# One core: products of probabilities and values taken one 64-key block at a time on the two halves of the array, with several moves of work between queues

## The chip, the core and the metric

The kernel runs on one core of a Trainium2 chip. The metric is the device time of one execution in microseconds (us). Before the change, three timed runs gave 854.46, 857.27 and 858.67 us, a median of 857.27 us. The profile is of one further execution, which took 856.18 us. The engines are called as in the profile: PE (matrix products; PEld is its weight load), DVE (vector), ACT (scalar), POOL (GpSimd) and SP, which here only issues DMAs and waits. "SPq" rows are what SP's own sequencer does, so a row `SPq L387 DMA_DIRECT2D` is the issue of one DMA, not its transfer.

## The reference, cut to what it computes

The input has 4096 tokens of 256 numbers (8 sequences of 512). First comes an attention over `ctx` in blocks of 64: a query sees only the 64 keys of its own block, in each of 16 heads of 16 numbers. Then comes a mixture of 8 experts, of which each token uses its best 2.

```python
x = x + _L0_xattn_ref(_layernorm(x, axis=-1), ctx_1024, ctx_1024, ...)
    scores = jnp.einsum('bhqd,bhkd->bhqk', q, k) / jnp.sqrt(jnp.float32(dk))
    bid = jnp.arange(s) // BLOCK_SIZE            # 64
    attn_mask = jnp.where(bid[:, None] == bid[None, :], 0.0, NEG)
    attn = jax.nn.softmax(scores + attn_mask, axis=-1)
    x = jnp.einsum('bhqk,bhkd->bhqd', attn, v)
    return x.transpose(0, 2, 1, 3).reshape(b, s, d) @ Wo + bo
x = x + _L0_ffn_ref(_layernorm(x, axis=-1), ...)
    weights = softmax(x @ gate_w.T + expert_bias); top_w, top_i = top_k(weights, 2)
    for e in range(8):
        h = gelu(x @ w_up[e].T); y = h @ w_down[e].T
        out = out + sparse_w[..., e:e+1] * y
    out = layernorm(out)
    return out + x
```

## The kernel before

**Two stages.** The tokens are 32 tiles of 128. The first stage is a pipeline over *steps*: in step i, each engine works on several tiles at once (the first number after `here(j, u, ...)` is the skew: tile i + skew). Steps 6 to 13 are a loop in hardware; the rest is written out. After the steps come 39 *items*: an item is 256 token rows of one expert, gathered through DRAM.

**One step on PE**, in order: transposes of the next tile (L452), scores of tile i (L464, on 64 rows at a time), transposes of the probabilities of tile i-1 (L474), the projections of q and k of tile i+1 (L486, L491), L499, the product of probabilities and values of tile i-1 (L507), the transposes of `xn2` of tile i-3 (L517), the projection of v of tile i (L529), the output projection (L544) and the gate's logits (L557).

L507 takes one pair of heads for both 64-key blocks of a tile at once: all 128 keys are contracted, and the values tile `v_x` holds each block's values in columns of its own, with zeros in the rows of the other block. Each product gives 66 columns, in fp32.

**One step on DVE**, in order: L807 (adds the output projection), L814 (statistics of the input tile i+3), L819, L825, L832, L839 (the second normalisation's mean and variance), L847 and L853 (maximum and difference of the scores), L861 and L869 (`xn` and `xn2`, two `tensor_scalar`), L878 (k for the next tile), L886 (`ctx_lo`, the low half of the context, which PE's L529 waits for), L893 and four L898 (division by the sum). In steps 15 to 33 parts of the routing follow (`route`).

**ACT** writes, among others, the scaled weights (L1007, L1022), `prob_t` (L1012), `ctx_hi` (L1017), q (L1031), the exponential (L1036) and the values into `v_x` (two L1059, one for each block).

**POOL** waits for L839, makes reciprocal roots (L1106, L1108), adds the output bias (L1136), makes L1140 and then the low half of a weight tile (L1144, 128x1024, which also waits for ACT's L1022), and later scatters rows (L1115).

**SP's queue**, one step: the input tile i+3 (L373, waited for by L814; here called the *x load*), the context and weights of tile i+1, row loads for the scatter, and the write of `xn2` of tile i-3 to `xn_rows` (L387, which waits for L869). SP issues in this order, and a wait holds everything behind it.

**Rows to the experts.** Each row of `xn_rows` has 256 numbers and, in column 256, the row's place. All 8192 places are written by one DMA on ACT's queue at the start (L987). For each tile, `row_in` loads two blocks of 128 rows from `xn_rows` into a ring of buffers `xr` (RING = 4), and POOL scatters each to `x_sorted`; a ring buffer is free again when its scatter has landed.

**The items.** The order of the items is decided in three rounds (tiles 0 to 10, 11 to 21, 22 to 31): item 0 may be loaded when the tiles up to 10 are scattered, item 3 when those up to 21 are, and item 7 when all are and nine blocks of zeros (the *pads*) are written. Item loads (L411), pads (L419, L420) and row loads (L367) all stand in SP's queue. On PE, `moe(k)` is: transposes of item k+2 (L572), `up` of item k+1 (L589, four quarters), `down` of item k (L605). A quarter of `up` for one item may be written when ACT's gelu (L1080) has read that quarter of the item before. The third round's counts (`read_counts(2)`, `place_rows(2)`, needed by the scatter of tiles 22 to 31) stand on DVE behind the four gelu quarters of item 0.

## Time and profile before

| what | before |
|---|---|
| profiled execution | 856.18 us, span of the trace 854.4 us |
| median of three timed runs | 857.27 us |
| PE busy | 734.5 us (86% of the span) |
| PEld busy | 655.7 us (77%) |
| DVE busy | 541.0 us (63%) |
| ACT busy | 389.6 us (46%) |
| POOL busy | 339.0 us (40%) |
| mean granted PE clock | 0.935 of full |

The span is the time from the first to the last instruction of the core; 1.8 us of the device time lie outside it. Busy shares are averages over stages with different limits, so they must be read by stretch. A group of the rows below gives the start in us, the duration in us, the engine, the line and the operation with its tiles; in square brackets stands how long the engine had been idle and what ended that.

### The profile page before, as it was taken

How to read it: one execution, taken by the hardware profiler on the slowest of the kernel's cores; microseconds unless marked ns; L12 is line 12 of the kernel's file. 1: busy time of each engine (PE TensorE's matmuls, PEld its weight loads, DVE VectorE, ACT ScalarE, POOL GpSimd, SP SyncE). 2: the span in 40 equal slices, each digit the busy share in tenths (PEclk: the TensorE clock that was granted, in tenths of full speed). 3: DMA queues.
4: the chain of work that ended last, by engine and by line, in shares of the span. 5: the costliest groups of instructions: out<-in, count | busy, mean ns of one | idle time of the engine just before them, and what ended most of it. 6: DMA issues, size and time to landing. Idle time of an engine off the chain costs nothing.

```text
span 854.4 us, 19926 instructions
## 1 busy us (share of the span) xinstructions
PE 734.5 (86%) x6340; PEld 655.7 (77%) x6340; DVE 541.0 (63%) x1292; ACT 389.6 (46%) x747; POOL 339.0 (40%) x500
## 2 busy tenths in 40 slices
PE   4788888889888888627968999999999999999990
PEld 4778887878777777416856998989988999999980
DVE  3576777786778777519425555555666667766662
ACT  3777778776667657212122222222333334433441
POOL 3344455444456455634535111111333334433453
PEclk9899999988989979858989999999999999999995
DMA  9234434333344553554673111112222233333222
GB/s 157 75 101 107 122 99 112 103 101 97 100 133 135 148 143 106 132 152 132 195 168 111 50 50 45 51 51 76 74 83 82 87 101 101 105 94 99 83 87 92
DMA packets 74090, 88.46 MB, mean 104 GB/s; under 512 B 15440, under 2 KB 64976, under 8 KB 74000
## 3 DMA queue, kind: packets, MB, share of 16 engines
q1 hardware_dynamic: 58112, 67.21, 29.2%
q0 software_dynamic: 6816, 18.65, 5.9%
q10 hardware_dynamic: 9072, 1.39, 1.8%
q8 instruction: 57, 0.93, 0.5%
q14 instruction: 33, 0.27, 0.1%
HBM read 53.63 MB, written 33.63 MB: 102 GB/s over the span
## 4 chain that ended last, share of the span: by engine, by line
PE 28%; issue 12%; POOL 9%; DMA 7%; SPq 2%; DVE 2%; ACT 0%; POOLq 0%; DVEq 0%
PE ps_a L589 13%; PE ps_b L605 13%; POOL y_rows L1176 4%; DMA area<-xn_rows 3%; DMA x_sorted<-area,slot_row 3%; POOL tiny L1163 2%; PE ps_c L572 1%; POOL x_sorted L1115 1%; DMA area<-x_sorted 1%; POOL tiny L1170 1%; POOL tiny L1165 1%; POOL tiny L1160 1%; DMA xn_rows<-area 1%; SPq L418 0%; SPq L419 0%
## 5 line engine op out<-in xcount | busy, mean ns | idle before, releaser
L589 PE MATMUL ps_a<-area,weights_s 128*128 128x256 f16 x1872 | 217.3, 277 | 1.9 <-DVE area L927 1.6
L605 PE MATMUL ps_b<-weights_s,area 128*128 x1872 | 210.6, 273 | 0.1
L589 PEld LDWEIGHTS ps_a<-area,weights_s 128*128 x1872 | 185.9, 100 | 26.6 <-issue 2.9
L605 PEld LDWEIGHTS ps_b<-weights_s,area 128*128 128x128 f16 x1872 | 183.1, 98 | 21.5 <-issue 0.3
L1080 ACT ACTIVATE area<-ps_a 128x512 f32<-128x512 f32 x156 | 92.6, 597 | 115.7 <-PE ps_a L589 112.7
L1176 POOL DMA_INDIRECT y_rows<-weights_s,tiny x78 | 85.9, 1101 | 127.3 <-ACT weights_s L1087 100.8
L1087 ACT ACTIVATE weights_s<-ps_b 128x512 f32<-128x512 f32 x39 | 23.3, 598 | 193.5 <-PE ps_b L605 165.6
L961 DVE SCALAR_TENSOR_TENSOR area<-area 128x512 f16<-128x512 f32 x156 | 108.0, 692 | 5.3
L1115 POOL DMA_INDIRECT x_sorted<-area,slot_row x64 | 66.2, 1034 | 54.3 <-DMA area<-xn_rows 41.2
L959 DVE TENSOR_SCALAR area<-area 128x512 f16<-128x512 f32 x156 | 66.5, 426 | 21.4 <-ACT area L1080 20.3
L1144 POOL TENSOR_TENSOR weights_s<-weights_s 128x1024 f16<-128x1024 f32 (+1 forms) x32 | 68.9, 2152 | 28.1 <-ACT weights_s L1022 27.8
L1106 POOL TENSOR_TENSOR area<-area,tiny 128x1 f32<-128x1 f32 x64 | 12.4, 193 | 149.9 <-DVE area L839 130.7
L925 DVE TENSOR_SCALAR area<-ps_c 128x512 f16<-128x512 f32 x39 | 26.9, 689 | 68.9 <-PE ps_c L572 68.9
L964 DVE SCALAR_TENSOR_TENSOR resid<-area,tiny,resid 128x256 f32<-128x256 f32 x32 | 15.5, 484 | 75.2 <-ACT resid L1092 75.0
L507 PE MATMUL ps_b<-area 128*128 128x66 f32 x512 | 61.0, 272 | 1.8 <-ACT area L1012 1.8
L507 PEld LDWEIGHTS ps_b<-area 128*128 128x128 f32 x512 | 59.7, 192 | 2.3 <-ACT area L1012 2.3
L1160 POOL TENSOR_TENSOR tiny<-tiny 128x1 f32<-128x1 f32 x32 | 7.5, 234 | 134.9 <-DVE tiny L975 134.9
L529 PE MATMUL ps_a<-area 128*128 128x256 f16 x192 | 30.1, 299 | 31.6 <-DVE area L886 31.6
L572 PE MATMUL ps_c<-cst,area 128*128 128x128 f32 x156 | 25.4, 289 | 31.6 <-DMA area<-x_sorted 31.6
L1031 ACT ACTIVATE area<-ps_c,tiny,cst 128x128 f32<-128x128 f32 x128 | 48.0, 460 | 6.4 <-PE ps_c L491 6.4
L878 DVE SCALAR_TENSOR_TENSOR area<-ps_c,cst 128x256 f32<-128x256 f32 x64 | 27.9, 477 | 36.3 <-issue 23.5
L529 PEld LDWEIGHTS ps_a<-area 128*128 128x128 f16 x192 | 17.5, 104 | 41.7 <-DVE area L886 39.1
(145 smaller groups left out, 1167.1 us busy)
## 6 DMA issues: line engine op xcount, KB each, us to landing
weights_s<-weights SPq DMA_DIRECT2D x32, 512.0 KB, 4.1
area<-x_sorted SPq DMA_DIRECT2D x39, 257.0 KB, 2.8
area<-xn_rows SPq DMA_DIRECT2D x64, 128.5 KB, 3.5
xn_rows<-area SPq DMA_DIRECT2D x32, 256.0 KB, 3.5
area<-y_rows SPq DMA_DIRECT2D x32, 256.0 KB, 2.9
resid<-x_in SPq DMA_DIRECT2D x32, 128.0 KB, 3.6
area<-ctx_t SPq DMA_DIRECT2D x32, 128.0 KB, 2.5
out<-resid SPq DMA_DIRECT2D x32, 128.0 KB, 2.8
```

The costliest lines, as they stand in the source:

```text
L507: mm = pe.matmul(ps_o[:, h // 4, (h % 4) * NB:(h % 4 + 1) * NB, :], prob_t[:, h, :], v_x[:, h // HC, h % HC, :, :], start=True, stop=True)
L529: mm = pe.matmul(ps_v, c[:, k, :], w[:, k, :], start=(n == 0), stop=(n == 3 * HC - 1))
L572: mm = pe.transpose(ps_x[:, b, at:at + P], xg[b][:, v, c * P:(c + 1) * P], ident)
L589: mm = pe.matmul(ps_h[:, q, (ic % 2) * SLOTS:(ic % 2 + 1) * SLOTS], weights_s[:, bass.ds(first + ((2 * hc + part) * WCOLS + ic * P), P)], ...
L605: mm = pe.matmul(ps_y[:, b, v * D:(v + 1) * D], g[b][:, ic, v * P:(v + 1) * P], weights_s[:, bass.ds(first + (col + part * WCOLS), D)], st ...
L959: dve.tensor_scalar(g_hi[b][:, c, :], src, G_SCALE, None, ALU.mult).then_inc(gh_r, 1)
L961: dve.scalar_tensor_tensor(g_lo[b][:, c, :], src, G_SCALE, g_hi[b][:, c, :], ALU.mult, ALU.subtract).then_inc(gl_r, 1)
L1031: act.activation(q_m[:, c, :, h, :], ps_q[:, c].rearrange("p (b q) -> p b q", b=NB), ACT.Identity, bias=bq_m[:, c, h:h + 1], scale=cst[:, ...
L1080: act.activation(g_s[q], ps_h[:, q, :], ACT.Gelu, scale=1.0 / (X_SCALE * W_SCALE)).then_inc(g_r, 1)
L1115: pool.indirect_dma_start(x_sorted[:, :], bass.IndirectOffsetOnAxis(ap=slot_row[:, m % TOPK, n:n + 1], axis=0), xr[s], None).then_inc(rsc[ ...
L1144: pool.tensor_tensor(w_part(t, 1), w_stage(t), w_part(t, 0), ALU.subtract).then_inc(w_lo_r, 1)
L1176: pool.indirect_dma_start(y_rows[:, :], bass.IndirectOffsetOnAxis(ap=y_at[k % 4][:, v:v + 1], axis=0), y_s[k % 2][:, v * D:(v + 1) * D], N ...
```

## The change

It has these parts.

1. L507's product is taken per block: 16 products of 64 keys and 33 columns instead of 8 of 128 keys and 66 columns, block 0 on the upper and block 1 on the lower 64 rows of the array, each into its own PSUM bank. `v_x` has half the columns and no zeros, so ACT fills it with one instruction in place of two (L1059), DVE divides with two 64x256 instructions in place of four 64x128 (L898), and the first memset is small.
2. `ctx_hi` (L1017) comes first in ACT's step, and `ctx_lo` (L886) moves on DVE from behind L878 to in front of L847.
3. The places of the rows are no longer written by one DMA at the start, but tile by tile: a DMA of 256 numbers of 4 bytes on SP's queue behind each L387.
4. The item loads move from SP's to ACT's queue (`load_item`), items 0 and 1 into step 34, and item k+4 between the second and third gelu of item k+1. SP issues all row loads up to tile 31 first, then the pads.
5. RING is 3, and the pads' zeros have a buffer of their own.

```diff
-RING = 4
+RING = 3
...
-        v_x = carve(PAIRS * NB * VCOLS).rearrange("p (s c b x) -> p s c b x", s=STRIPS, c=HC, b=NB)
+        v_x = carve(PAIRS * VCOLS).rearrange("p (s c x) -> p s c x", s=STRIPS, c=HC)
...
+        pad_zero = carve(ROW)
...
                 for m, s, uses in loads_of(n):
                     since(sp, rsc[s], 16 * uses)
-                    if m == 0:
-                        sp.wait_ge(at_out, 16)
-                    sp.wait_ge(xn2_out[n % 2], 16 * (n // 2 + 1))
+                    sp.wait_ge(xn2_out[n % 2], 32 * (n // 2 + 1))
...
                     sp.dma_start(xn_by_tile.rearrange("(c t) p d -> t p c d", c=TOPK)[bass.ds(t, 1), :, :, 0:D].rearrange("a p c d -> p (a c) d"),
                                  xn2.unsqueeze(1).to_broadcast([P, TOPK, D])).then_inc(xn2_out[b], 16)
+                    sp.dma_start(xn_by_tile.rearrange("(c t) p d -> t p c d", c=TOPK)[bass.ds(t, 1), :, :, D:ROW].rearrange("a p c d -> p (a c) d"),
+                                 route_consts[:, R_AT:R_END].rearrange("p (c t) -> t p c", c=TOPK)[bass.ds(t, 1)].rearrange("a p c -> p (a c)").unsqueeze(2),
+                                 allow_slow_non_contiguous=True).then_inc(xn2_out[b], 16)
...
-            x_units = x_sorted.rearrange("(s v p) d -> s p v d", v=SUBS, p=P)
+            for n in range(17, TILES):
+                row_in(n)
...
             def moe(k):
-                i = k + 4
-                if item_valid(i):
-                    b = i % 2
-                    if i in ROUND_OF:
-                        r = ROUND_OF[i]
-                        sp.wait_ge(items_r, r + 1)
-                        rows_scattered(sp, sum(ROUNDS[r][0:2]))
...
-                for n in {-2: (17, 18, 19, 20, 21), -1: (22, 23), 0: (24, 25, 26), 1: (27, 28, 29, 30, 31)}.get(k, ()):
-                    row_in(n)
...
                     for h in range(PAIRS):
-                        mm = pe.matmul(ps_o[:, h // 4, (h % 4) * NB:(h % 4 + 1) * NB, :], prob_t[:, h, :],
-                                       v_x[:, h // HC, h % HC, :, :], start=True, stop=True)
+                        for n in range(NB):
+                            r = slice(n * BLOCK, (n + 1) * BLOCK)
+                            mm = pe.matmul(ps_o[:, n, h, :], prob_t[r, h, :], v_x[r, h // HC, h % HC, :], start=True, stop=True)
...
                 t, half, b = here(j, u, 0)
                 if valid(t):
+                    dve.wait_ge(ctx_hi_r, t + 1)
+                    since(dve, v_ps, t)
+                    dve.scalar_tensor_tensor(ctx_lo, ctx[b], CTX_SCALE, ctx_hi, ALU.mult, ALU.subtract).then_inc(ctx_lo_r, 1)
+
+                t, half, b = here(j, u, 0)
+                if valid(t):
                     since(dve, sub_r, t)
...
-            act.dma_start(xn_rows.rearrange("(g p) d -> p g d", p=P)[:, :, D:ROW], route_consts[:, R_AT:R_END].unsqueeze(2),
-                          allow_slow_non_contiguous=True).then_inc(at_out, 16)
...
+            def load_item(i):
+                b = i % 2
+                if i in ROUND_OF:
+                    r = ROUND_OF[i]
+                    act.wait_ge(items_r, r + 1)
+                    rows_scattered(act, sum(ROUNDS[r][0:2]))
+                    if r == 0:
+                        act.wait_ge(k_ps, TILES)
+                    if r == 2:
+                        act.wait_ge(padded, 16 * (E + 1))
+                since(act, gt_ps, i - 1)
+                since(act, at_r, i - 1)
+                at_x = act.value_load(item_x[0:1, i:i + 1], min_val=0, max_val=SPARE)
+                act.dma_start(xg[b], x_units[bass.ds(at_x, 1)].rearrange("a p v d -> p (a v) d")).then_inc(xgot[b], 16)
...
+                if isinstance(j, int) and 2 * j + u == 34:
+                    load_item(0)
+                    load_item(1)
...
                     for q in range(GQ):
+                        if q == 2 and item_valid(k + 4):
+                            load_item(k + 4)
                         act.wait_ge(h_ps, GQ * i + 1 + q)
```

Line numbers of the changed kernel differ by a few from those of before. In SP's queue, in the written-out steps, this stood between the write of `xn2` (L387) and the x load of the next step (L373):

```order
L377 DMA area<-ctx_t 128x256
L381 DMA weights_s<-weights 128x1024
L387 DMA xn_rows<-area 128x2x256
L373 DMA resid<-x_in 128x256
L377 DMA area<-ctx_t 128x256
```

and this stands there now (L385 is the write of `xn2`, L387 the DMA of the places, L371 the x load):

```order
L375 DMA area<-ctx_t 128x256
L379 DMA weights_s<-weights 128x1024
L385 DMA xn_rows<-area 128x2x256
L387 DMA xn_rows<-route_consts 128x2x1
L371 DMA resid<-x_in 128x256
L375 DMA area<-ctx_t 128x256
```

One DMA has come between the two, and nothing else. On DVE, one step before, from L839 on:

```order
L839 BN_AGGR area<-area 128x2
L847 TENSOR_REDUCE area<-ps_a 128x16
L853 TENSOR_TENSOR area<-ps_a,area 128x1024
L861 TENSOR_SCALAR area<-resid,area 128x256
L869 TENSOR_SCALAR area<-resid,area,rs_all 128x256
L878 SCALAR_TENSOR_TENSOR area<-ps_c,cst 128x256 x2
L886 SCALAR_TENSOR_TENSOR area<-area 128x256
L893 RECIPROCAL area<-ps_b 128x16
L898 TENSOR_TENSOR area<-ps_b,area 64x128 x4
```

and the same step now (L820 is the former L839, L828 the former L886, L856 the former L869):

```order
L820 BN_AGGR area<-area 128x2
L828 SCALAR_TENSOR_TENSOR area<-area 128x256
L834 TENSOR_REDUCE area<-ps_a 128x16
L840 TENSOR_TENSOR area<-ps_a,area 128x1024
L848 TENSOR_SCALAR area<-resid,area 128x256
L856 TENSOR_SCALAR area<-resid,area,rs_all 128x256
L865 SCALAR_TENSOR_TENSOR area<-ps_c,cst 128x256 x2
L874 RECIPROCAL area<-ps_b 128x16
L878 TENSOR_TENSOR area<-ps_b,area 64x256 x2
```

`ctx_lo` has moved in front of the two score operations, so that one more instruction stands between the former L839, for which POOL waits, and the former L869. On ACT, from the loading of gelu's table on, the first items now read so (L1078 is a gelu quarter, L983 and L984 an item load; the first load there is item 2's, the next item 3's, the last item 4's):

```order
L1065 ACT_TABLE_LOAD
L1065 ACTIVATE tiny<-tiny 128x1
L983 TENSOR_LOAD item_x
L983 ISA x2
L984 ISA
L984 DMA area<-x_sorted 128x2x257
L1078 ACTIVATE area<-ps_a 128x512 x2
L983 TENSOR_LOAD item_x
L983 ISA x2
L984 ISA
L984 DMA area<-x_sorted 128x2x257
L1078 ACTIVATE area<-ps_a 128x512 x4
```

Before, the gelu quarters of items 0 and 1 stood there with nothing between them, and ACT had no item load:

```order
L995 ACTIVATE area<-area 128x80
L1071 ACT_TABLE_LOAD
L1071 ACTIVATE tiny<-tiny 128x1
L1080 ACTIVATE area<-ps_a 128x512 x8
L1087 ACTIVATE weights_s<-ps_b 128x512
L1080 ACTIVATE area<-ps_a 128x512 x4
```

## Rows read from the trace of the kernel before

**Rows 1.** Windows: us; busy PE, PEld, DVE, ACT, POOL; PE clock, DMA share, GB/s.

```profile
600.00:700.00 100.00, 100.00 (x918) 90.03 (x916) 64.63 (x139) 35.55 (x65) 32.74 (x57) 1.00 0.29 86
```

**Rows 2.** Timeline of PE, from 92 to 102 us (steps of the loop).

```profile
92.14 0.83 PE L529 MATMUL ps_a<-area 128*128 128x256 f16 x6 [1.10 <-DVE area L886]
...
94.38 1.16 PE L464 MATMUL ps_a<-area 64*128 64x128 f32 x16
...
98.41 1.90 PE L507 MATMUL ps_b<-area 128*128 128x66 f32 x16
100.15 0.39 PE L517 MATMUL ps_a<-cst,area 128*128 128x128 f32 x2
101.64 0.83 PE L529 MATMUL ps_a<-area 128*128 128x256 f16 x6 [1.11 <-DVE area L886]
```

**Rows 3.** Timeline of DVE, the same steps.

```profile
94.98 0.43 DVE L814 BATCH_NORM_STATS2 area<-resid 128x6 f32 x1 [0.17 <-DMA resid<-x_in]
...
96.06 0.18 DVE L839 BATCH_NORM_AGGREGATE area<-area 128x2 f32<-128x6 f32 x1 [0.17 <-issue]
...
98.89 0.41 DVE L869 TENSOR_SCALAR area<-resid,area,rs_all 128x256 f32 x1
...
101.11 0.48 DVE L886 SCALAR_TENSOR_TENSOR area<-area 128x256 f16<-128x256 f32 x1
```

**Rows 4.** Timeline of SP's queue, the same steps.

```profile
89.87 0.41 SPq L387 DMA_DIRECT2D xn_rows<-area  x1
90.51 0.35 SPq L373 DMA_DIRECT2D resid<-x_in  x1
```

**Rows 5.** Timeline of POOL, the same steps.

```profile
96.32 0.19 POOL L1106 TENSOR_TENSOR area<-area,tiny 128x1 f32<-128x1 f32 x1 [4.52 <-DVE area L839]
...
99.17 2.13 POOL L1144 TENSOR_TENSOR weights_s<-weights_s  x1
```

**Rows 6.** Timeline of ACT, the same step.

```profile
97.53 0.41 ACT L1017 ACTIVATE area<-area 128x256 f16<-128x256 f32 x1
```

**Rows 7.** Timeline of DVE, 262 to 284 us (written-out steps with routing).

```profile
264.15 2.22 DVE L869 TENSOR_SCALAR area<-resid,area,rs_all 128x256 f32<-128x256 f32 x1
...
270.49 0.43 DVE L814 BATCH_NORM_STATS2 area<-resid 128x6 f32<-128x256 f32 x1 [0.39 <-DMA resid<-x_in]
```

**Rows 8.** Timeline of POOL, the same stretch.

```profile
264.01 2.20 POOL L1144 TENSOR_TENSOR weights_s<-weights_s 128x1024 f16<-128x1024 f32 x1
```

**Rows 9.** Timeline of SP's queue, the same stretch.

```profile
266.40 0.40 SPq L387 DMA_DIRECT2D xn_rows<-area  x1
```

**Rows 10.** Groups by line and shape: busy us, mean ns, idle before.

```profile
L869 DVE TENSOR_SCALAR area<-resid,area,rs_all 128x256 f32<-128x256 f32 x24 | 22.5, 940 | 3.2 <-POOL rs_all L1108 1.9 <-DMA xn_rows<-area 1.3
```

**Rows 11.** DMA queues of the page: packets, MB, share of 16 engines over the span.

```profile
q10 hardware_dynamic: 9072, 1.39, 1.8%
```

**Rows 12.** Timeline of PE, transposes of items 0, 3 and 7.

```profile
377.76 1.09 PE L572 MATMUL ps_c<-cst,area 128*128 128x128 f32 x4 [15.55 <-DMA area<-x_sorted]
...
405.91 1.12 PE L572 MATMUL ps_c<-cst,area 128*128 128x128 f32 x4 [5.72 <-DMA area<-x_sorted]
...
466.06 0.60 PE L572 MATMUL ps_c<-cst,area 128*128 128x128 f32 x4
```

**Rows 13.** Timeline of SP's queue, row loads of tiles 13 to 16, and pads.

```profile
360.81 11.45 SPq L367 DMA_DIRECT2D area<-xn_rows  x8
...
420.27 9.61 SPq L419 DMA_DIRECT2D x_sorted<-weights_s  x8
```

**Rows 14.** Chain that ended last, 388 to 402 us: row loads and scatters in turn.

```profile
388.84 2.38 DMA area<-xn_rows
...
391.48 5.40 DMA x_sorted<-area,slot_row
396.90 2.23 DMA area<-xn_rows
...
399.40 2.60 DMA x_sorted<-area,slot_row
```

More of the change, by code:

```diff
@@ L471, in step @@
                     pe.wait_ge(p_r, t + 1)
-                    since(pe, o_r, 4 * t)
+                    since(pe, o_r, 2 * t)
                     for h in range(PAIRS):
@@ L514, in rows_for_gate @@
                         since(pe, x2t_r, t)
-                        since(pe, v_r, 2 * (min(t + 3, TILES) if isinstance(t, int) else t + 3))
+                        since(pe, v_r, min(t + 3, TILES) if isinstance(t, int) else t + 3)
                         for c in range(HC):
@@ L524, in step @@
                     pe.wait_ge(ctx_lo_r, t + 1)
-                    since(pe, v_r, 2 * t)
+                    since(pe, v_r, t)
                     n = 0
@@ L645, in _ @@
         def _(dve):
-            dve.memset(v_x, 0.0).then_inc(zeroed, 1)
-            dve.wait_ge(zeroed, 1)
-            for n in range(NB):
-                r = slice(n * BLOCK, (n + 1) * BLOCK)
-                ins = dve.memset(v_x[r, :, :, n, 2 * DK:VCOLS].rearrange("p s c x -> p (s c) x"), 1.0)
-            ins.then_inc(zeroed, 1)
+            dve.memset(v_x.rearrange("p s c x -> p (s c) x")[:, :, 2 * DK:VCOLS], 1.0).then_inc(zeroed, 1)
             links = [0]
@@ L866, in step @@
                     dve.wait_ge(rs2_r, t + 1)
-                    since(dve, xn2_out[1 - b], 16 * (half + b))
+                    since(dve, xn2_out[1 - b], 32 * (half + b))
                     since(dve, x2t_ps, t)
@@ L880, in step @@
                                                  ALU.add, ALU.mult).then_inc(k_r, 1)
-                t, half, b = here(j, u, 0)
-                if valid(t):
-                    dve.wait_ge(ctx_hi_r, t + 1)
-                    since(dve, v_ps, t)
-                    dve.scalar_tensor_tensor(ctx_lo, ctx[b], CTX_SCALE, ctx_hi, ALU.mult, ALU.subtract).then_inc(ctx_lo_r, 1)
                 t, half, b = here(j, u, -1)
@@ L997, in step @@
             def step(j, u):
+                t, half, b = here(j, u, 0)
+                if valid(t):
+                    act.wait_ge(ctx_in[b], 16 * (half + 1))
+                    since(act, v_ps, t)
+                    act.activation(ctx_hi, ctx[b], ACT.Copy, scale=CTX_SCALE).then_inc(ctx_hi_r, 1)
                 t, half, b = here(j, u, 1)
@@ L1012, in step @@
                     act.activation(prob_t, ps_pt, ACT.Copy).then_inc(pt_r, 1)
-                t, half, b = here(j, u, 0)
-                if valid(t):
-                    act.wait_ge(ctx_in[b], 16 * (half + 1))
-                    since(act, v_ps, t)
-                    act.activation(ctx_hi, ctx[b], ACT.Copy, scale=CTX_SCALE).then_inc(ctx_hi_r, 1)
                 t, half, b = here(j, u, 0)
@@ L1056, in step @@
                     since(act, o_ps, t)
[L1057 to L1061 removed]
+                    act.activation(v_x[:, :, :, 0:2 * DK], ps_v.rearrange("p (c s d) -> p s c d", c=HC, s=STRIPS),
+                                   ACT.Copy, scale=1.0 / (CTX_SCALE * W_SCALE)).then_inc(v_r, 1)
             step(-1, 1)
```

46 lines of the change are left out of this document (15 added, 31 removed).

## The prediction

> **What bounds the kernel now.** The windows come first. In the items, PE is busy for all of a stretch of 100 us [rows 1]; an item costs it 100 records (48 up, 48 down, 4 transposes), so 918 records in 100 us are 10.9 us an item, and nothing in the change touches that work. What can move is the attention stage (to about 360 us), the passage to the items (360 to 466 us), and, where they end later or sooner, the end by as much.
>
> The timelines of one step come next, engine by engine. On PE a step of the loop takes 9.50 us (92.14 to 101.64), and 1.11 us of it is a wait for L886 [rows 2]. PE's own part is thus 8.39 us. A second circle runs beside it. SP writes `xn2` (L387 at 89.87), and behind it issues the x load (90.51) [rows 4]; L814 begins at 94.98, and its bracket says that it waited for that load, 5.11 us after L387's issue [rows 3]. From L814 to L839 are 1.08 us, from L839 to L869 2.83 us [rows 3], then 0.41 us for L869 itself and some 0.1 us until SP issues the next L387. The sum is 5.11 + 1.08 + 2.83 + 0.41 + 0.1 = 9.5 us. **Two circles of the same length bound a step**, and the change shortens only the first.
>
> In the passage I read PE's transposes. Item 0's came at 377.76 after 15.55 us of waiting for its rows, item 3's at 405.91 after 5.72 us, and from item 7's, at 466.06, PE runs on [rows 12]. SP issued the row loads of tiles 13 to 16 from 360.81 to 372.3, with item 0's load behind them, and from 420.27 spent 9.61 us on pads [rows 13].
>
> **The change, part by part.** *PE's product.* L507 takes 1.74 us from its start to L517's (98.41 to 100.15), for 16 records on the full array [rows 2]. The new form has 32 records on half the rows. Bounds: if pairs run side by side, no more than now; if they follow each other like the 16 records of L464 (1.16 us, also on 64 rows), 2.32 us, 0.6 more. I take +0.4. PE's circle is then 8.8 us without the wait for L886. This is hidden as long as the other circle is longer; without that cover it costs 0.4 us a step.
>
> *`ctx_lo` earlier.* L886 no longer holds PE. On DVE it now stands between L839 and L869, so the second circle gets longer by its place: 0.48 us as it stands at 101.11 [rows 3], 0.3 if the part in which it waited is taken off. I take 0.4.
>
> *The places, tile by tile.* The new DMA stands between L387 and the x load, so the x load is issued later by one issue; L387 to the x load was 0.64 us [rows 4], which is the upper bound, and nothing is the lower one, if the x load waits for L387's data anyway. Its 256 packets go over 16 engines. ACT's queue, with 9072 packets, nearly all of this kind, used 1.8% of 16 x 854.4 us [rows 11], at most 27 ns each, so 16 packets take 0.43 us. Together 0.4 to 1.1 us; I take 0.7. The Trainium skill (DMA: Bandwidth & Descriptors, section Queues, rings and completion order) says that a DMA's semaphore increment lands only after every earlier write of that engine; by it the x load could not be seen before the 4-byte writes are done, the upper end of this term. No row here has both DMAs, so the sum goes by 0.7.
>
> So the second circle becomes 9.5 + 0.4 + 0.7 = 10.6 us against 9.5. In the 8 steps of the loop that is 1.1 x 8 = **+9 us** (5.5 to 12). In the written-out steps with an x load and without routing (4, 5, 14 to 16) SP needs fewer instructions of its own; I take 0.8 x 5 = **+4** (0 to 6). In the 12 with routing DVE's own work mostly covers the x load (one waited 0.39 us [rows 7]); I take **+2** (0 to 10).
>
> *L869 against L1144.* In a step at 264 us POOL's L1144 began at 264.01 [rows 8] and L869, at 264.15, took 2.22 us in place of 0.41 [rows 7]. L869's 24 written-out instances are busy 22.5 us [rows 10]: (22.5 - 24 x 0.41) / 1.81 = 7 such cases. Where L869 begins first, as at 98.89 against 99.17 [rows 3, 5], it is not held. The Trainium skill (SBUF — State Buffer, section Who interferes with whom) states the rule: one port pair is shared by the two, and whichever starts first keeps it for the whole instruction. The trace agrees, with 0.14 us one way and 0.28 the other. What becomes of the 0.28 us? L869 moves back by 0.4 (L886 in front). L1144 moves forward by 0 to 0.3, where it waited for L1022, since L1017 (0.41 us [rows 6]) no longer stands ahead of that. And L886 now reads at the time of POOL's L1106, 0.26 us behind L839 [rows 3, 5], which can push POOL's chain back by 0 to 0.4. L1144 thus begins between 0.42 before and 0.28 behind L869, nearer to before. I take 11 of the 17 written-out steps with an x load, where 6 were held. A held L869 delays L387 and so the x load by 1.8, of which 1.5 is left: 5 x 1.5 = **+7.5** (from -11, all gone, to +28, all 25 steps).
>
> *Start and end of the stage.* Nine steps without such an x load lose their wait for L886, at most 1.1 us each; DVE and ACT follow closely, so I take half: **-4** (-10 to 0).
>
> *The passage.* Item 0's load now waits only for tile 10, so PE can begin at about 362.2 (377.76 - 15.55). But item 3's load stands on ACT in front of item 0's third gelu and holds it until all tiles up to 21 are scattered. A ring buffer's turn (load, scatter) took 8.04 us (388.84 to 396.88) and 5.10 us (396.90 to 402.00) [rows 14]; I take the mean, 6.6, with three buffers 2.2 us a block. The 18 blocks of tiles 13 to 21 from 361.3 end near 402. PE then stands in the middle of `up` of item 1; half an `up` (2.6), a `down` (5.2) and 1.5 to get going put item 3's transposes at 411.5, against 405.91. Further, DVE's third counts stand behind the same gelu, about 7.5 us later by the lengths of the instructions between, so the scatter of tile 22 begins at 409.5. Of its 20 blocks three are loaded already and 17 follow at 2.2: SP is done at 447. The pads come after that (10 us of issues, 5 to land): item 7 can be loaded at 462. ACT waits for it in front of item 4's third gelu, so half an `up`, a `down` and the cold start, 10.5 us, lie ahead of item 7's transposes: 472.5 against 466.06, **+6.5**. With turns of 5.10 throughout it is -11, with 8.04 +23.
>
> *At nothing.* One ACT and two DVE instructions fewer a tile lie beside the x load. The 39 item loads on ACT, about 1 us each, are covered in the items, where ACT is busy 35.55 of 100 us [rows 1]; without that cover they would hold gelu. The memset and the DMA of places at the start have no engine waiting for them in the first steps.
>
> **Sum**, against the profiled 856.2 us: 856.2 + 9 + 4 + 2 + 7.5 - 4 + 6.5 = 881.2. The median of the runs lies 1.1 us above the profiled one, so about **882**.
>
> **Rivals.** *The x load is in time* (faster). The second circle is the time from L387 to the x load's landing, plus 0.4 + 1.08 + 2.83 + 0.41 + 0.1 = 4.8. If the landing takes 4.0 us, places included, PE's 8.8 bounds. In favour: at 270.49 L814 saw the load 4.09 us after the L387 of 266.40 [rows 7, 9]; against: 5.11 in the loop [rows 3, 4]. Then 13 steps gain 0.7 (-9), the 12 with routing 0.3 for the shorter DVE (-4), the ends -4, the passage stays at +6.5, and no held L869 is added: 845.7, or **847**. It decides from a landing of 4.7 us downward, where the circle falls under 9.5.
>
> *L869 is held everywhere* (much slower), also in the loop: 25 held instead of 6 give 19 x 1.5 = 28.5 in place of 7.5, **903**. In favour: the order above; against: in the loop L1144 was bounded by POOL's own chain, which L886 can only push back.
>
> *It nets out* (same). Landing at 4.7 and a ring that turns in 6 us: no term of the steps but -4, and the passage at +4: **857**.
>
> **Chances.** The forecast 0.57 (867 to 894, by its terms' bounds), x load in time 0.17, all held 0.13, nets out 0.13. Half a per cent, 4.3 us, is about what a measurement of this kernel can tell from no change. So faster 0.17, same 0.13, slower 0.70. The range for 8 in 10 is 850 to 896: it takes in "nets out", all of the forecast but its edge, and the nearer parts of the two outer cases.
>
> **What would show it.** Right: L814's idle time named by the x load in most steps of the loop; no wait of L529 for L886's successor; loop steps of 10.2 to 11 us; more than 7 L869 over 2 us; PE's transposes of item 0 near the end of the stage, then a gap of some 25 us before the middle of item 1's `up`, ended by ACT. Wrong: L814 without waits and steps of 9 us; or a gap in item 1 so short that item 7's transposes come no later after the stage's end than before (106 us).

## The result, and the profile after

The changed kernel takes 917.56 us (median of 4 runs, 915.03 to 919.65), the kernel before 857.97 us in the same session. The ratio is 1.0695 [1.0646, 1.0745]: about 60 us slower, where 25 us were forecast. The profiled execution after has a span of 917.8 us against 854.4, 63 us more.

I divide these 63 us by two instants of each trace. The last `xn2` copy (L869, now L856) ends at 359.97 us before and at 409.18 after: **the attention stage lost 49 us** (forecast 18.5). From there to the transposes of item 7 were 106.1 us and are now 120.4: **the passage lost 14 us** (forecast 6.5). From item 7 on both kernels need 388 us.

Windows after, columns as in [rows 1], and two windows of before beside them:

```profile
42.00:190.00 148.00, 125.17 (x1096) 110.29 (x1095) 97.25 (x192) 85.72 (x168) 55.12 (x86) 0.82 0.39 86
190.00:360.00 170.00, 146.43 (x1268) 129.89 (x1266) 126.17 (x292) 100.17 (x196) 75.79 (x108) 0.81 0.47 106
600.00:700.00 100.00, 100.00 (x918) 90.04 (x917) 57.77 (x116) 30.43 (x54) 22.65 (x34) 1.00 0.21 63
```

```profile
42.00:190.00 148.00, 128.71 (x1141) 117.19 (x1142) 110.08 (x291) 113.89 (x228) 68.25 (x106) 0.98 0.38 107
190.00:360.00 170.00, 142.08 (x1109) 126.11 (x1106) 129.77 (x351) 107.76 (x216) 87.18 (x125) 0.89 0.45 123
```

The items are untouched (918 records in 100 us, as in [rows 1]). In the attention stage DVE, ACT and POOL are busy for less of the same time. PE is busy for nearly as long as before, but its granted clock (third number from the right) is 0.82 and 0.81 where it was 0.98 and 0.89.

One step of the loop on DVE after, then POOL and SP's queue in the same stretch (compare [rows 3 to 5]):

```profile
115.68 0.18 DVE L820 BATCH_NORM_AGGREGATE area<-area 128x2 f32<-128x6 f32 x1 [0.17 <-issue]
...
117.39 1.22 DVE L840 TENSOR_TENSOR area<-ps_a,area 128x1024 f32<-128x1024 f32 x1
118.53 2.33 DVE L848 TENSOR_SCALAR area<-resid,area 128x256 f32 x1
120.78 0.40 DVE L856 TENSOR_SCALAR area<-resid,area,rs_all 128x256 f32 x1
...
127.76 0.43 DVE L795 BATCH_NORM_STATS2 area<-resid 128x6 f32 x1 [2.25 <-DMA resid<-x_in]
...
129.03 0.43 DVE L828 SCALAR_TENSOR_TENSOR area<-area 128x256 f16<-128x256 f32 x1
129.37 1.22 DVE L834 TENSOR_REDUCE area<-ps_a 128x16 f32<-128x1024 f32 x1
130.62 1.22 DVE L840 TENSOR_TENSOR area<-ps_a,area 128x1024 f32<-128x1024 f32 x1
```

```profile
117.75 0.73 POOL L1132 TENSOR_TENSOR resid<-resid,area 128x256 f32 x1
118.43 0.20 POOL L1136 TENSOR_TENSOR mr_all<-area,rs_all 128x1 f32 x1
118.57 2.13 POOL L1140 TENSOR_TENSOR weights_s<-weights_s  x1
```

```profile
121.34 0.41 SPq L385 DMA_DIRECT2D xn_rows<-area  x1
122.02 0.62 SPq L387 DMA_DIRECT2D xn_rows<-route_consts  x1
123.48 0.35 SPq L371 DMA_DIRECT2D resid<-x_in  x1
```

The same copy before, and the small POOL instruction that ran beside it:

```profile
98.57 0.41 DVE L861 TENSOR_SCALAR area<-resid,area 128x256 f32 x1
```

```profile
98.69 0.34 POOL L1140 TENSOR_TENSOR mr_all<-area,rs_all 128x1 f32 x1
```

The step is 13.23 us long (117.39 to 130.62). L848, the former L861, takes 2.33 us in place of 0.41, and ends 0.16 us behind POOL's L1140 (120.86 and 120.70). The x load is issued 2.14 us behind L385, with the places between them, and L795 waits 2.25 us for it: 6.42 us after L385 instead of 5.11 [rows 3, 4].

Groups by line and shape over the whole execution (busy us, mean ns, idle before), with PE's two below:

```profile
L848 DVE TENSOR_SCALAR area<-resid,area 128x256 f32<-128x256 f32 x24 | 30.5, 1273 | 0.0
L856 DVE TENSOR_SCALAR area<-resid,area,rs_all 128x256 f32<-128x256 f32 x24 | 18.6, 774 | 5.6 <-DMA xn_rows<-route_consts 3.7 <-POOL rs_all L1104 1.9
L848 DVE TENSOR_SCALAR area<-resid,area 128x256 f32 x8 | 12.8, 1603 | 0.0
L795 DVE BATCH_NORM_STATS2 area<-resid 128x6 f32<-128x256 f32 x24 | 10.2, 425 | 32.2 <-DMA resid<-x_in 25.1 <-issue 7.0
L795 DVE BATCH_NORM_STATS2 area<-resid 128x6 f32 x8 | 3.4, 427 | 11.8 <-DMA resid<-x_in 11.8
```

```profile
L494 PE MATMUL ps_b<-area 64*128 64x33 f32 x1024 | 65.4, 279 | 1.8 <-ACT area L1011 1.8
L503 PE MATMUL ps_a<-cst,area 128*128 128x128 f32 x64 | 17.8, 369 | 49.8 <-DVE area L856 49.8
```

Of the 64 copies of L848 and L856, 23 took over 1 us, 17 of them L848; before it was 8 of 64, seven of them L869 [rows 10]. PE now waits 49.8 us for L856, in front of L503. Its wait for the `ctx_lo` copy, in front of L515, is gone.

The passage: PE's transposes of items 0, 3 and 7; SP's queue; the item loads and what follows on ACT.

```profile
411.83 1.08 PE L558 MATMUL ps_c<-cst,area 128*128 128x128 f32 x4 [0.42 <-issue]
...
462.25 0.60 PE L558 MATMUL ps_c<-cst,area 128*128 128x128 f32 x4
...
529.60 0.60 PE L558 MATMUL ps_c<-cst,area 128*128 128x128 f32 x4
```

```profile
410.78 88.92 SPq L365 DMA_DIRECT2D area<-xn_rows  x38
500.77 9.39 SPq L404 DMA_DIRECT2D x_sorted<-area  x8
510.20 0.47 SPq L405 DMA_DIRECT2D x_sorted<-area  x1
```

```profile
451.18 0.39 ACTq L984 DMA_DIRECT2D area<-x_sorted  x1
451.61 2.06 ACT L1078 ACTIVATE area<-ps_a 128x512 f32<-128x512 f32 x4 [31.12 <-issue]
...
517.60 0.39 ACTq L984 DMA_DIRECT2D area<-x_sorted  x1
```

Item 0 starts 2.7 us after the stage, where 2.2 were forecast, and then ACT stands 31 us in front of item 3's load. The pads leave only behind all 38 row loads, and item 7's load (517.60) behind the pads.

### The profile page after: what moved, and what is told of

The parts are those of the page before. It is cut to its first block, busy times and chain, and to the rows that moved or that the text cites. A ratio compares the mean times of both kernels' runs of the same rounds, so it can differ in the third digit from the quotient of the medians.

```text
span 917.8 us, 20908 instructions
## 1 busy us (share of the span) xinstructions
PE 773.6 (84%) x6852; PEld 685.9 (75%) x6852; DVE 562.7 (61%) x1226; ACT 377.3 (41%) x715; POOL 337.7 (37%) x500
## 4 chain that ended last, share of the span: by engine, by line
PE 26%; issue 12%; DMA 9%; POOL 8%; DVE 2%; SPq 1%; ACT 0%; ACTq 0%; POOLq 0%; DVEq 0%
PE ps_b L591 12%; PE ps_a L575 12%; POOL y_rows L1172 4%; DMA x_sorted<-area,slot_row 4%; DMA area<-xn_rows 4%; POOL tiny L1159 1%; PE ps_c L558 1%; POOL tiny L1166 1%; DMA x_sorted<-area 1%; POOL tiny L1161 1%; POOL tiny L1156 1%; POOL x_sorted L1111 1%; SPq L403 0%; DVE area L856 0%; SPq L404 0%
## 5 line engine op out<-in xcount | busy, mean ns | idle before, releaser
L1078 ACT ACTIVATE area<-ps_a 128x512 f32<-128x512 f32 x156 | 90.3, 596 | 176.7 <-PE ps_a L575 68.4
L1172 POOL DMA_INDIRECT y_rows<-weights_s,tiny x78 | 84.8, 1087 | 142.6 <-ACT weights_s L1083 118.4
L1102 POOL TENSOR_TENSOR area<-area,tiny 128x1 f32<-128x1 f32 x64 | 16.7, 260 | 202.9 <-DVE area L820 185.0
L1111 POOL DMA_INDIRECT x_sorted<-area,slot_row x64 | 63.5, 993 | 58.7 <-DMA area<-xn_rows 38.4
L1140 POOL TENSOR_TENSOR weights_s<-weights_s 128x1024 f16<-128x1024 f32 (+1 forms) x32 | 68.4, 2136 | 19.6 <-ACT weights_s L1016 19.4
L494 PEld LDWEIGHTS ps_b<-area 64*128 64x128 f32 x1024 | 61.7, 193 | 7.2 <-issue 4.8
L494 PE MATMUL ps_b<-area 64*128 64x33 f32 x1024 | 65.4, 279 | 1.8 <-ACT area L1011 1.8
L943 DVE SCALAR_TENSOR_TENSOR resid<-area,tiny,resid 128x256 f32<-128x256 f32 x32 | 15.5, 484 | 75.3 <-ACT resid L1088 75.2
L503 PE MATMUL ps_a<-cst,area 128*128 128x128 f32 x64 | 17.8, 369 | 49.8 <-DVE area L856 49.8
L1011 ACT ACTIVATE area<-ps_b 128x1024 f32<-128x1024 f32 x32 | 32.8, 1024 | 45.2 <-PE ps_b L459 45.2
L530 PE MATMUL ps_a<-area 128*128 128x256 f32 x128 | 48.0, 515 | 1.0 <-ACT area L1041 1.0
L449 PE MATMUL ps_a<-area 64*128 64x128 f32 x512 | 47.3, 337 | 1.7 <-issue 1.7
```

The costliest lines, as they stand in the source:

```text
L449: mm = pe.matmul(ps_a[:, a].rearrange("p (s x k) -> p x s k", s=2, k=BLOCK)[:, c * NB + n], q_m[r, c, n].rearrange("p h q -> p (h q)"), k_ ...
L494: mm = pe.matmul(ps_o[:, n, h, :], prob_t[r, h, :], v_x[r, h // HC, h % HC, :], start=True, stop=True)
L530: mm = pe.matmul(ps_wo_last if last_out(t) else ps_wo, o_t[:, h, :], wo_s[:, h, :], start=(h == 0), stop=(h == 1))
L1078: act.activation(g_s[q], ps_h[:, q, :], ACT.Gelu, scale=1.0 / (X_SCALE * W_SCALE)).then_inc(g_r, 1)
L1111: pool.indirect_dma_start(x_sorted[:, :], bass.IndirectOffsetOnAxis(ap=slot_row[:, m % TOPK, n:n + 1], axis=0), xr[s], None).then_inc(rsc[ ...
L1140: pool.tensor_tensor(w_part(t, 1), w_stage(t), w_part(t, 0), ALU.subtract).then_inc(w_lo_r, 1)
```

## The experiments

Each ratio is to runs of the kernel before on the same chip, so it is the ratios that are compared between chips. "Held" counts the copies to `xn` and `xn2` that took over 1 us, of 64; "stage" is the end of the last copy to `xn2`; "cold" is the number of the 32 steps in which the four records of PE's output projection (L530 in the changed kernel) took over 1.4 us together, up to 2.1, instead of 1.0 to 1.1; "passage" is as above. These four come from one execution of each kernel. Executions of one kernel differ: the kernel before took 846.1 to 856.8 us on one chip, and the one traced took 856.2. So a few us between two traces show nothing by themselves.

| kernel | ratio to before | held | stage | cold | passage |
|---|---|---|---|---|---|
| before | 1 | 8 | 360.0 | 6 | 106.1 |
| changed | 1.0695 [1.0646, 1.0745] | 23 | 409.2 | 18 | 120.4 |
| `e1_places` | 1.0435 [1.0383, 1.0486] | 28 | 386.7 | 15 | 114.2 |
| `e2_ctx` | 1.0484 [1.0395, 1.0573] | 15 | 389.7 | 12 | 114.2 |
| `e3_both` | 1.0305 [1.0250, 1.0359] | 6 | 371.9 | 13 | 116.8 |
| `e4_poolwait` | 1.0167 [1.0107, 1.0226] | 1 | 362.9 | 10 | 112.6 |
| `e7_halves` | 1.0131 [1.0049, 1.0213] | 8 | 377.3 | 13 | 105.7 |
| `e5_xearly` | 1.0261 [1.0161, 1.0362] | 27 | 373.6 | 12 | 120.4 |
| `a_both` | 0.9864 [0.9788, 0.9941] | 1 | 330.6 | 2 | 120.4 |
| `e9_passage` | 1.0186 [1.0108, 1.0263] | 9 | 359.9 | 4 | 119.0 |
| `c_pads` | 0.9701 [0.9635, 0.9766] | 1 | 316.9 | 1 | 115.2 |
| `c_cures_sp` | 0.9491 [0.9441, 0.9541] | 1 | 315.1 | 2 | 102.1 |
| `b_both` | 0.9971 [0.9935, 1.0007] | 0 | 358.2 | 7 | 102.9 |
| `b_poolwait` | 0.9987 [0.9952, 1.0022] | 0 | 354.2 | 7 | 102.2 |

**Parts 2 and 3 undone, apart and together.** Part 3 undone takes the second DMA out and puts the one at the start back:

```diff
-                    sp.dma_start(xn_by_tile...[bass.ds(t, 1), :, :, D:ROW]..., ...).then_inc(xn2_out[b], 16)
...
+            act.dma_start(xn_rows...[:, :, D:ROW], route_consts[:, R_AT:R_END].unsqueeze(2), ...).then_inc(at_out, 16)
```

> The changed kernel (917.6 us) with part 3 undone: the places again in one DMA at the start on ACT's queue. Theory 1 (the port: what was lost in the attention stage is mostly that L848 or L856 is held by POOL's L1140, in 20 steps against 8 before, 1.9 us each, because ctx_lo now stands in front of L834): the x load lands 0.7 us sooner in each of 24 steps, and the held steps stay, 20 of 32 within 4: 897 to 905. Theory 2 (the late x load: the stage was lengthened by the second DMA between the xn2 write and the x load): 25 to 35 us come back, 883 to 893, and the idle time of L795 for the x load falls from 36.9 us to under 8.

Part 2 undone moves the blocks of `ctx_lo` (here) and `ctx_hi` back, without a change in them:

```diff
-                    dve.scalar_tensor_tensor(ctx_lo, ctx[b], CTX_SCALE, ctx_hi, ALU.mult, ALU.subtract).then_inc(ctx_lo_r, 1)
...
                     dve.tensor_reduce(row_max, ps_s, AX.X, ALU.max).then_inc(max_r, 1)
...
+                    dve.scalar_tensor_tensor(ctx_lo, ctx[b], CTX_SCALE, ctx_hi, ALU.mult, ALU.subtract).then_inc(ctx_lo_r, 1)
...
                     dve.wait_ge(o_ps, t + 1)
```

> The changed kernel with part 2 undone: ctx_hi behind prob_t on ACT and ctx_lo behind L878 on DVE, as before. Theory 1 (the port): held copies fall from 20 to about 8, and the path from L795 to L856 loses the 0.43 us of ctx_lo: 12 x 1.9 + 24 x 0.4 = 32 us back, 882 to 892. Theory 2 (the late x load): only the 0.4 us per step come back, 905 to 912, and the held copies stay about as many. PE waits for ctx_lo again in both.

`e3_both` has both edits.

> The changed kernel with parts 2 and 3 undone, so with the product by halves, the item loads on ACT and the ring of three. Both theories: the attention stage is as long as before within 5 us (last L856 at 355 to 365 us), and what is left over 858 is the passage, 14 us: 866 to 876. If it stays over 880, the product by halves costs in the attention stage too.

`e1_places` gave back 2.6% (some 22 us), between the two theories; `e2_ctx` gave back 2.1% (18 us), less than theory 1 wanted. The counts say why neither explains the loss alone. With `ctx_lo` in front of L834 and the old places, 28 copies are held, nearly one in every step; with the new places and `ctx_lo` at its old place still 15; with both undone 6. **Each part by itself brings copies under L1140**: 28 and 15 are held, and 6 with neither part. Together they give back 3.9%, and the rest, 1.0305, lies above what both theories allowed (866 to 876 us, at most 1.021): the stage is still 12 us longer, and PE cold in 13 steps, with nothing left of the change in it but the half product. That led to `e7_halves`.

**The port alone.** POOL's L1140 is made to wait until DVE is through L856; nothing is undone.

```diff
                     pool.wait_ge(w_hi_r, t + 1)
+                    since(pool, xn2_r, t - 2)
```

> The changed kernel, all parts kept, with one wait more: POOL's L1140 (the low part of a weight slice) waits for L856 of the same step, so that it never runs beside L848 and L856. Theory 1 (the port): none of the 64 copies is held any more, up to 20 x 1.9 = 38 us back, of which some is eaten where PE or the x load bounds the step next: 880 to 895. Theory 2 (the late x load): a held copy only uses up time in which the x load would be waited for anyway, so under 8 us come back: 910 to 918.

From 1.0695 to 1.0167, some 45 us, more than the 38 expected; between the two profiled executions the stage is 46 us shorter (409.2 to 362.9). Theory 2, by which under 8 us come back, is out. But the x load is late here too: L795 still waits for it 21 times, 41.5 us in all. One step of the loop on DVE, and POOL's instruction that now comes behind L856:

```profile
119.03 0.40 DVE L848 TENSOR_SCALAR area<-resid,area 128x256 f32 x1
119.35 0.41 DVE L856 TENSOR_SCALAR area<-resid,area,rs_all 128x256 f32 x1
...
125.73 0.43 DVE L795 BATCH_NORM_STATS2 area<-resid 128x6 f32 x1 [0.79 <-DMA resid<-x_in]
...
129.66 0.40 DVE L848 TENSOR_SCALAR area<-resid,area 128x256 f32 x1
```

```profile
120.12 2.13 POOL L1141 TENSOR_TENSOR weights_s<-weights_s  x1 [0.98 <-DVE area L856]
```

The step is 10.63 us (119.03 to 129.66). The prediction's sum of the second circle, held copies left out, was 10.6.

**The x load a step earlier**, so that it no longer stands behind the `xn2` write and the places:

```diff
-                t, half, b = here(j, u, 3)
+                t, half, b = here(j, u, 4)
                 if valid(t):
                     since(sp, x_in[b], 16 * half)
...
-            for i in range(-3, 0):
+            for i in range(-4, 0):
```

> The changed kernel, all parts kept, with each x load issued one step earlier, ahead of the xn2 write and the places instead of behind them. Theory 1 and 2 together (the circle through the x load is what bounds a step): L795 no longer waits for it (36.9 us before), and the step falls to the circle of L856, L503, L530, L543, L788 and L795, 4.4 + 6.5 = 10.9 us where a copy is held: 25 to 35 us less than the changed kernel, ratio to before 1.03 to 1.04. If the x load's lateness were only what fills a wait on PE, under 8 us come back.

1.0261, a little better than expected: L795 waits twice for the x load, 4.3 us in all. A copy is still held in 27 cases, and a step of the loop is 10.64 us (L848 at 100.18 and 110.82), near the 10.9 expected of the circle through L503. The late x load was real: 36 us of the stage (409.2 to 373.6), not much less than the 46 of the other cure. The trace is of the longest of the four executions, 884.0 us against 870.1 to 882.6, so 36 may be too little.

**Both cures together**, the edits of the last two kernels:

> The changed kernel, all parts kept, with both cures: L1140 waits for L856 of its step, and the x load is issued a step earlier. Theory 1 and 2: no copy is held and L795 does not wait for the x load; a step is bound by PE (8.8 us at full clock, more where the clock falls) or by the circle through L503 and L795, 4.4 + 4.7 = 9.1 us. 28 steps of 9.1 to 9.8 us against 10.4 with the first cure alone: 20 to 35 us less than that, ratio to before 0.98 to 0.99, the passage (+6 to +14 us) included.

0.9864, as expected, and the first version that is faster than the kernel before, by 1.4% [0.6%, 2.1%]. The two cures nearly add up, 79 us of the stage (409.2 to 330.6) against 46 + 36. That fits the held copy and the late load standing one behind the other on the same circle.

**The half product alone**, in the kernel before. The cut shows PE's lines; the rest of part 1 comes with them (`v_x` without zeros, one copy of values on ACT and two divisions on DVE):

```diff
-                        mm = pe.matmul(ps_o[:, h // 4, (h % 4) * NB:(h % 4 + 1) * NB, :], prob_t[:, h, :],
-                                       v_x[:, h // HC, h % HC, :, :], start=True, stop=True)
+                        for n in range(NB):
+                            r = slice(n * BLOCK, (n + 1) * BLOCK)
+                            mm = pe.matmul(ps_o[:, n, h, :], prob_t[r, h, :], v_x[r, h // HC, h % HC, :], start=True, stop=True)
```

> The kernel before with part 1 alone (the product by halves). Theory 3 (the half product costs PE its clock): with parts 2 and 3 undone the stage was still 12 us longer than before, and PE's L514 to L542 ran at half the clock in every second step of the loop; so here too every second step is about 11 us instead of 9.5, and the kernel is 10 to 20 us slower than before, with a granted clock of about 0.91 in the attention stage against 0.98. Rival (the half product is hidden, as predicted): same as before within 4 us, clock 0.98.

Slower by 1.3% [0.5%, 2.1%], some 11 us. Between the two spans it is 17 us; the traced run of this kernel is the longest of its four. The v projection of the step before, one step on PE, and windows of 2 us over the same place (columns as in [rows 1]):

```profile
106.56 0.83 PE L530 MATMUL ps_a<-area 128*128 128x256 f16 x6 [0.79 <-DVE area L882]
...
112.92 1.98 PE L509 MATMUL ps_b<-area 64*128 64x33 f32 x32
114.82 0.44 PE L518 MATMUL ps_a<-cst,area 128*128 128x128 f32 x2
116.06 1.46 PE L530 MATMUL ps_a<-area 128*128 128x256 f16 x6 [0.79 <-DVE area L882]
117.31 1.92 PE L545 MATMUL ps_a<-area 128*128 128x256 f32 x4
```

```profile
113.00:115.00 2.00, 2.00 (x34) 1.96 (x34) 0.75 (x3) 2.00 (x6) 1.61 (x2) 1.00 0.21 74
115.00:117.00 2.00, 1.21 (x7) 0.73 (x7) 1.94 (x6) 1.15 (x3) 0.71 (x1) 0.69 0.73 89
117.00:119.00 2.00, 2.00 (x7) 1.60 (x6) 0.07 (x1) 0.66 (x2) 0.00 (x0) 0.50 0.29 59
119.00:121.00 2.00, 2.00 (x24) 1.69 (x23) 1.25 (x5) 0.94 (x2) 0.00 (x0) 0.96 0.92 280
```

The product itself takes 1.90 us to the next line's start, 0.16 more than the 1.74 of [rows 2]. But behind the 0.79 us wait for `ctx_lo`, shorter than the 1.11 us of before [rows 2], the granted clock is 0.50, its lower level of 1.2 GHz, until about 119 us, and L545 takes 1.92 us. Nearly every second step of the loop is so, 11 us instead of 9.5. In the step between, the same wait of 0.79 us leaves L530 at 0.83 us, so the length of this wait alone does not decide it.

**The passage alone**, parts 4 and 5 in the kernel before (ring, `pad_zero`, order on SP, and the loads on ACT):

```diff
-RING = 4
+RING = 3
...
+            for n in range(17, TILES):
+                row_in(n)
...
-            moe_steps(-4, moe)
+            moe_steps(0, moe)
...
+                        if q == 2 and item_valid(k + 4):
+                            load_item(k + 4)
```

> The kernel before with parts 4 and 5 alone: item loads on ACT's queue, all row loads first, three ring buffers, pad_zero of its own. The attention stage is untouched but for the ring (last L869 within 3 us of 360). From there to the transposes of item 7 were 106 us before, 112.6 to 120.4 in the changed kernel and its variants: 112 to 117 here, so 6 to 11 us slower than before. If the longer passage came from the longer attention stage (scatters not done by its end), it is within 3 us of before.

The stage ends where it did (359.9), and the passage is 119.0: 12.9 us more, above the 6 to 11 expected. So the longer passage does not come from the longer stage.

**What in the passage.** With both cures, the pads moved between the row loads of tiles 23 and 24:

```diff
-            for n in range(17, TILES):
+            for n in range(17, 24):
                 row_in(n)
+            sp.wait_ge(pad_r, 2)
...
+            for n in range(24, TILES):
+                row_in(n)
```

> The changed kernel with both cures (the wait in front of L1140, the x load a step earlier), and the pads on SP's queue between the row loads of tiles 23 and 24 instead of behind those of tile 31. Theory 4 (the passage is long because item 7's load waits for the pads, and these stand behind all row loads): the load of item 7 no longer waits 10 us of pads and 6.5 us of landing after the last row, so the transposes of item 7 come 106 to 112 us after the last L856 instead of 120.4: 8 to 14 us less than with the cures alone, ratio to before 0.970 to 0.977. Rival (the ring of three sets the passage): the row loads end later by as much as the pads are earlier, and the ratio stays at 0.986 within 0.004.

And parts 4 and 5 undone, with both cures in:

> The changed kernel with both cures, and parts 4 and 5 undone: item loads again on SP's queue between the row loads, the pads in the middle, four ring buffers. The passage is 104 to 108 us again instead of 120.4: 12 to 16 us less than with the cures alone, ratio to before 0.967 to 0.973. If the passage is instead bound by the scatters' own number (all 20 blocks of tiles 22 to 31 are due whatever the order), under 5 us come back: 0.98 or more.

`c_pads` measures 0.9701, inside the range expected, but by luck. The passage is 115.2, 5.2 us less than in `a_both` and not 8 to 14. Even these 5.2 are not shown to come from the pads, since the eight kernels with the change's parts 4 and 5 have passages from 112.6 to 120.4. The other gain of `c_pads` over `a_both`, 14 us, lies in the stage (330.6 to 316.9), whose code is the same in both: a longer wait here and there, and a cold PE behind it, as at 181 us in `a_both`, where PE waited 2.00 us for a context load. What set it off stays open; the two also ran on different chips. With all of parts 4 and 5 undone the passage is 102.1, 18 us less, where 12 to 16 were expected. The ratio, 0.9491, lies well below the 0.967 to 0.973 expected, because the stage is shorter than in `a_both` here as well (315.1). What is clear is the step from these eight passages to the 102.1 to 106.1 of the five kernels with parts 4 and 5 as before. How it divides between the pads' place, the ring of three and ACT's wait in front of gelu was not taken apart.

**The cures without the change**, the same edits: the first alone, and both, in the kernel before.

> The kernel before with the first cure alone, the wait of L1144 for L869 of its step. Theory 1: none of the 8 held copies is left, and the x load is 1.8 us less late in those steps: 9 to 15 us faster than before, ratio 0.982 to 0.990. Theory 2 (the port costs little by itself): the same within 4 us.

> The kernel before with both cures and nothing of the change. Its 8 held copies go (8 x 1.85 = 15 us), the x load is no longer waited for, and a step stays at PE's 9.5 us with the wait for L886. Theories 1 and 2: 12 to 18 us faster than before, ratio 0.979 to 0.986, so that parts 1 to 3 with the cures are worth 8 to 12 us (against the run with the cures and parts 4 and 5 undone). If the held copies cost nothing before, the same within 4 us.

Both miss: the held copies are gone (0 of 64), and nothing is gained, 0.9987 and 0.9971. L1144's successor (L1145) has not stopped colliding; it meets another instruction. The rows show `ctx_lo` on DVE (L886, 42 to 360 us) before and then with the first cure, one such case on DVE, POOL's instruction, and PE behind it:

```profile
L886 DVE SCALAR_TENSOR_TENSOR area<-area 128x256 f16<-128x256 f32 x30 | 13.0, 433 | 0.0
```

```profile
L886 DVE SCALAR_TENSOR_TENSOR area<-area 128x256 f16<-128x256 f32 x30 | 21.6, 718 | 0.0
```

```profile
112.36 1.08 DVE L886 SCALAR_TENSOR_TENSOR area<-area 128x256 f16<-128x256 f32 x1
```

```profile
111.02 2.13 POOL L1145 TENSOR_TENSOR weights_s<-weights_s  x1 [1.14 <-DVE area L869]
```

```profile
113.49 1.46 PE L529 MATMUL ps_a<-area 128*128 128x256 f16 x6 [1.70 <-DVE area L886]
```

The `ctx_lo` copy ends 0.29 us behind L1145 (113.44 and 113.15), PE waits 1.70 us for it instead of 1.11, and runs cold (1.46 us in place of 0.83 [rows 2]). The Trainium skill (SBUF — State Buffer, section Who interferes with whom) says that an instruction of DVE with two inputs in SBUF also contends with POOL's reads; L886 has two, and 0.72 us against 0.43 in the mean agrees.

The rival is that the 8 held copies cost nothing before, which would also leave the time the same. The traces speak against it: between the loop and the last step with an x load, where 6 of the 8 were held, `b_poolwait` needs 133.3 us and `b_both` 136.5 in place of 142.2; in the loop, where none was, they need 81.3 and 82.8 in place of 75.9, and there `ctx_lo` takes 0.69 us or more in each of the eight steps of `b_poolwait`. That the two cancel is read from these traces; no run frees `ctx_lo` in the kernel before.

In `c_cures_sp` `ctx_lo` stands in front of L834, and what DVE does under L1140 then is k and the attention output, both read from PSUM; no `ctx_lo` copy takes over 0.49 us. There all of parts 1 to 3 stay in, PE's clock from 42 to 190 us is 1.00, and the kernel is 5.1% faster than before.

```profile
42.00:190.00 148.00, 146.48 (x1534) 130.85 (x1532) 116.67 (x290) 119.34 (x234) 77.13 (x119) 1.00 0.47 117
```

## Why the prediction was wrong

The direction was right, the size was not: 917.6 against 882, outside the range of 850 to 896. The step that failed is the one headed "L869 against L1144". It asked for too few held copies at too low a price, since it took POOL's chain in the loop as something that L886 "can only push back".

- **The held copies (+7.5 forecast).** I asked only whether L869 would fall under L1144, and took 5 more cases, none of them in the loop, where POOL's chain was to leave L1144 behind. In truth it is mostly the copy ahead of it, L861's successor, that is caught, at 118.53 against 118.57, in the loop too. The two copies stand so close together that the later start of one only hands the collision to the other.

  In the loop L1144 began 0.60 us after L861 before (99.17 [rows 5] and 98.57), and L1140 0.04 after L848 now. Measured from L839 and its successor (96.06 [rows 3] and 115.68), the copy moved back by 0.34 us, as L886's place wanted, but POOL's instruction moved forward by 0.22: the small one ahead of it, which had run beside L861 for 0.34 us, now takes 0.20. Of the 25 steps that have an x load behind their `xn2` write, 19 have a held copy, 13 more than the 6 of before, not 5. With the collision taken away the stage falls from 409.2 to 362.9, so the term forecast at 7.5 measures 46 us, 2.1 for each of 22 copies in place of 1.5. It is not measured cleanly: what would be left of the 8 cases of before goes too, and PE is cold in 10 steps in place of 18. The rival "held everywhere" (903) had the mechanism, and I gave it 0.13.

  The Trainium skill's rule that whichever starts first keeps the port (SBUF — State Buffer, section Who interferes with whom), on which I leaned, is not refuted by 118.53 against 118.57: DVE's L840 runs to 118.61, and if L848's work begins only then, it begins behind L1140's start. All fourteen traces fit that. They have 220 copies that overlap POOL's long instruction, leaving out 14 that began in its last 0.5 us. In the 128 held ones POOL began at most 0.005 us behind the end of DVE's record before; in the 92 others it began 0.003 us or more behind it. So the start of a copy's own record, which overlaps the one before by some 0.08 us, does not tell who was first, and the end of the record before does.
- **The loop's circle (+9).** Right in what it names, and in its sum by luck. The changed loop gained 24 us in 8 steps, 12.5 us each (starts of `xn2`, 80.9 to 181.0); without the held copies 8 steps of the loop took 10.8 us on average in `e4_poolwait` (`xn2` from 76.6 to 162.7) against 10.6 forecast. But the 5.11 us were read from one step. On the mean of the loop's eight steps the x load landed 4.3 us behind the issue of the `xn2` write before, and 5.7 in the changed kernel and in `e4_poolwait`. So the places cost about 1.4 us and not 0.7, the circle through the x load was the shorter one before, some 8.9 us by the same terms, and the two errors cancel. That is past the upper end of 1.1 that the prediction gave the term, and the way of that end, a load seen only behind the 4-byte writes, fits the trace: in all 25 steps of the changed kernel that have both DMAs, the x load landed 0.15 to 0.93 us behind the places, mostly 0.17. L795 did wait for the x load, 22 times and 36.9 us, and the earlier load in `e5_xearly` took that away.
- **The product (+0.4, hidden).** The duration was sized at +0.4, within its bounds, and measures +0.16. The error is the word hidden: I costed its time and not what it does to the clock. Alone part 1 costs 1.3%, 17 us between the traces, all of it in the stage, through steps at 0.50 of the clock. That the fall comes with part 1 is shown by `e7_halves`, which differs from the kernel before in that part alone (13 cold steps against 6, and 4 to 7 in the other kernels with the old product). That it is the product is argued: it is all that differs in PE's own work, and ACT's and DVE's shorter work can reach PE only through its waits, of which the one for `ctx_lo` became shorter. Why that product lets the clock fall, no run shows; with that wait gone it hardly falls, 2 cold steps in `c_cures_sp`.
- **The end of the stage (-4).** From the last step with an x load to the end were 61.5 us and are 70.0, so +8.5: PE's wait for L886 went, as said, but copies are held here too (L848 took 2.24 us at 352.73), and in three of the last steps PE's L515 is cold (1.49 us in place of 0.82). The steps between the loop and that point, with routing, lost 15.5 us, the start of the stage 1.0. That the 15.5 lie near the 4 + 2 + 7.5 forecast for these steps is luck: in `e4_poolwait`, without held copies, the same stretch took 135.6 us, 22 less than in the changed kernel and 7 less than before.
- **The passage (+6.5).** 14.3 in the changed kernel, 12.9 alone, and from 6.5 up over the eight kernels that have it. To item 3's load the working held: its load came 42.4 us after the stage's last copy began (451.18 - 408.77), as worked out. Behind it three terms were short. From tile 22's first scatter (458.86) to the end of the row loads (499.70) were 40.8 us for 17 blocks, 2.4 each in place of 2.2, with POOL's scatters of the items' results (L1172) in between; from there to item 7's load, with the pads, 17.9 us instead of 15; and from that load to its transposes 12.0 us instead of 10.5. Together 7.7 of the 7.8 us.

The parts add up nearly as ratios: the product 1.3% and the passage 1.9% make 3.2%, where `e3_both`, which has just these, measured 3.05%. Parts 2 and 3 add 1.3% and 1.7% to that when each is alone, and 3.8% together; the intervals of these runs, 0.5% to 0.9% to either side, leave the 1.3 and 1.7 undistinguished.

## What to carry to other kernels

When a change moves a copy on DVE by a few tenths of a microsecond, look for every instruction near it that shares a port with a long one on POOL, not for the one that was caught last time; and order the two by a wait, behind which only instructions on PSUM follow, instead of leaving it to chance. A wait on the path of the engine that bounds a step costs more than its length where the engine's clock falls behind it: here the four records of the output projection then took 1.9 us instead of 1.0. A load that no buffer holds back belongs ahead of the write that waits, where its lateness bounds a step; in the kernel before, where it did not, the same move gained nothing. And a term of a circle that is read from one step should be read from several.

## What was not expected of the hardware

With 32 products on 64 rows in place of 16 on 128, and what belongs to them on ACT and DVE, the granted clock between 42 and 190 us went from 0.98 to 0.91, though the product takes only 0.16 us more and the wait behind it is shorter (0.79 against 1.11 us). And a wait added on POOL to keep it out of the way of two copies made a third instruction on DVE take up to 1.80 us instead of 0.43 in the mean; removing 8 collisions of some 1.8 us gained nothing.
